# Start-up of a fused Fourier-mixing kernel: second weights loaded on ScalarE's queue, maxima found with TensorE, residual map moved, paired evacuations

## What is computed

```python
def _L0_conv_ref(x, w1, b1, w2, b2, bias_w, bias_b):      # x: (8, 32, 32, 384)
    bias = x @ bias_w.T + bias_b
    xb = x.reshape(B, H, W, nb, bs)                       # nb = 4 blocks of bs = 96 channels
    xf = jnp.fft.rfftn(xb, axes=(1, 2), norm='ortho')
    xr, xi = (xf.real, xf.imag)
    r1 = relu(_block_mul(xr, w1[0]) - _block_mul(xi, w1[1]) + b1[0])
    i1 = relu(_block_mul(xr, w1[1]) + _block_mul(xi, w1[0]) + b1[1])
    r2 = _block_mul(r1, w2[0]) - _block_mul(i1, w2[1]) + b2[0]
    i2 = _block_mul(r2, w2[1]) + _block_mul(i1, w2[0]) + b2[1]
    out = jnp.fft.irfftn(jax.lax.complex(r2, i2), s=(H, W), axes=(1, 2), norm='ortho')
    return out.reshape(B, H, W, C) + bias

x = x + _L0_conv_ref(_gn(x), ...)     # _gn: group norm, 32 groups, over pixels and channels of the group
```

## Time and profile before

| | |
|---|---|
| median of three runs | 462.18 us |
| the profiled execution, its own time | 459.74 us |
| its span, first to last instruction | 457.6 us |
| PE busy | 400.7 us (88%) |
| DVE busy | 344.6 us (75%) |
| ACT busy | 227.7 us (50%) |
| POOL busy | 66.5 us (15%) |

### The profile page before, as it was taken

The page is one execution under the profiler, slowest core; times in us unless marked ns, Lnnn a source line. Parts: engine busy times, 40 slices in busy tenths (PEclk is TensorE's granted clock), DMA queues, the critical chain, the costliest instruction groups (busy, mean ns, idle before and its releaser), DMA issues.

```text
span 457.6 us, 19262 instructions
## 1 busy us (share of the span) xinstructions
PE 400.7 (88%) x8530; PEld 355.4 (78%) x8530; DVE 344.6 (75%) x768; ACT 227.7 (50%) x504; POOL 66.5 (15%) x72
## 2 busy tenths in 40 slices
PE   4529778899899998999899998999899998995896
PEld 4418667787788988988788988988788887984794
DVE  3676988887797788868688788768787778769324
ACT  2632765326644476427643566437642575435320
POOL 0000007600060005100150006000240007000000
PEclk9758999999999999999999999999999999998899
DMA  6770000053001700052001700151002600130003
GB/s 212 212 210 0 4 1 4 2 184 130 3 5 36 278 4 4 26 178 112 4 4 50 265 4 4 35 208 73 5 3 94 221 3 4 37 140 1 4 4 138
DMA packets 12566, 33.22 MB, mean 73 GB/s; under 512 B 4994, under 2 KB 6692, under 8 KB 12484
## 3 DMA queue, kind: packets, MB, share of 16 engines
q1 hardware_dynamic: 12484, 32.00, 20.1%
HBM read 16.26 MB, written 12.58 MB: 63 GB/s over the span
## 4 chain that ended last, share of the span: by engine, by line
PE 62%; DVE 22%; issue 4%; SPq 4%; ACT 4%; DMA 2%; DVEq 0%
PE bank L552 62%; DVE r L1066 2%; DMA bias_all<-in_bias_b 2%; DVE rsum L1059 2%; DVE xs L1006 2%; DVE xs L1008 2%; DVE z L991 2%; DVE xs L1004 1%; DVE dev L1022 1%; DVE dev L1024 1%; SPq L511 1%; DVE sX L1020 1%; SPq L506 1%; DVE rho L991 1%; DVE g L1073 1%
## 5 line engine op out<-in xcount | busy, mean ns | idle before, releaser
L552 PE MATMUL bank<-biasw,y 128*64 128x384 f16 x1152 | 112.5, 339 | 4.5 <-DVE g L1073 4.4
L552 PEld LDWEIGHTS bank<-biasw,y 128*64 128x64 f16 x1152 | 94.2, 196 | 7.8 <-issue 5.2
L552 PE MATMUL bank<-w2s,rho 128*64 128x96 f16 x3072 | 83.9, 208 | 0.2 <-issue 0.2
L552 PEld LDWEIGHTS bank<-w2s,rho 128*64 128x64 f16 x3072 | 80.8, 109 | 3.6 <-issue 2.8
L907 ACT ACTIVATE z<-bank 128x384 f16<-128x384 f32 x72 | 35.2, 489 | 65.7 <-PE bank L552 65.0
L552 PE MATMUL bank<-w1R,y 128*128 128x192 f16 (+3 forms) x768 | 59.6, 228 | 1.6 <-issue 1.1
L552 PE MATMUL bank<-tab,x_sb 128*128 128x128 f32 x384 | 52.5, 290 | 9.6 <-DMA x_sb<-in_x 5.8
L991 DVE SCALAR_TENSOR_TENSOR z<-bank,z 128x384 f16<-128x384 f32 x72 | 40.0, 557 | 26.3 <-ACT z L907 25.9
L552 PEld LDWEIGHTS bank<-tab,x_sb 128*128 128x128 f32 x384 | 48.2, 201 | 14.3 <-issue 8.0
L892 ACT ACTIVATE g<-bank 128x384 f16<-128x384 f32 x64 | 31.0, 484 | 55.8 <-PE bank L552 55.7
L991 DVE SCALAR_TENSOR_TENSOR rho<-bank,rho 128x256 f16<-128x256 f32 (+2 forms) x128 | 40.1, 364 | 23.8 <-ACT rho L925 15.4
(11 more groups left out here) (104 smaller groups left out, 464.4 us busy)
## 6 DMA issues: line engine op xcount, KB each, us to landing
x_sb<-in_x SPq DMA_DIRECT2D x16, 768.0 KB, 6.8
out<-o_sb SPq DMA_DIRECT2D x14, 768.0 KB, 3.5
y<-y SPq DMA_DIRECT2D x24, 128.0 KB, 2.8
out<-o_sb SPq DMA_DIRECT2D x8, 192.0 KB, 1.9
tab<-in_tab SPq DMA_DIRECT2D x1, 672.0 KB, 5.8
o_sb<-in_bias_wt SPq DMA_DIRECT2D x4, 144.0 KB, 2.8
b1s<-in_b1h SPq DMA_DIRECT2D x1, 384.0 KB, 5.0
tab<-in_tab SPq DMA_DIRECT2D x1, 291.5 KB, 2.7
```

What stands on the lines that cost most here:

```text
L552: return nc.tensor.matmul(o, lhsT, rhs, start=start, stop=stop, **kw)
```

## The change

1. The twelve loads of `w2` are issued by ACT, ahead of its first activation. Nothing of them is left on SP's queue. `w2real` is zeroed first, so that these loads can start with those of `w1`.
2. POOL takes no part in the scales. DVE reduces to one number in each partition (`peak`), a PE product with the identity lays the 128 numbers in a row of PSUM (`peak_to_row`), DVE finds the scale in partition 0, and a PE product with ones gives it to all partitions (`top_to_all`). The constants grow by the identity, 128 columns.
3. The second maxima, the second scale and all of `second_forms` are made in the start: part 0 ahead of the first maximum, part 1 and `second_peak` ahead of `moments(0)`, `second_scales` between `scales(0)` and `y_low`.
4. The map is made inside `c1` of image 0: `shift_rows` after unit 1, the PE products ahead of unit 6, `shift_all` after unit 6.
5. POOL's `add_map(b)` waits for `scales` of image b + 1 instead of the end of `p4`, and does one image each time, image b itself (images 6 and 7 together).
6. `spectrum_sum`, `r_high` and `r_low` take two neighbouring units in one instruction where they can. All units have 128 rows; `p3_half` gets three more matmuls for that.
7. In `p4` the third `c2_bias` moves from ahead of `j` = 6 to ahead of `j` = 7.

```diff
-            sp.wait_ge(w1_zeroed, 1)
+            sp.wait_ge(w1_zeroed, 2)
...
-            sp.wait_ge(zeroed, N_ZERO)
-            with nc.allow_non_contiguous_dma(reason="one column of 96 per block"):
-                for dst, src in w2_loads():
-                    sp.dma_start(dst, src).then_inc(w2_in, 16)
...
                 if m == 0 and not first:
                     pe.wait_ge(o_ready, 8 * b)
+                    pe.wait_ge(added_ready, 6)
...
                     if u == 6:
+                        if first:
+                            pe.wait_ge(shift_in, 16 * N_SHIFT)
+                            pe.wait_ge(added_ready, 1)
+                            mm(y_bank[1][:, 0:CH], T("impulse", 2), b2rows[:, :], True, False, skip_group_check=True)
+                            for blk in range(BLOCKS):
+                                last = mm(y_bank[1][:, BC * blk:BC * blk + BC], b2row0[:, blk, :], w2imag[:, blk, :], False, blk == BLOCKS - 1, skip_group_check=True)
+                            last.then_inc(shift_prod, 1)
                         p3_half(b, 0, first)
...
-                        for slot in range(3 if t == 3 else 4):
+                        for slot in range(4):
...
-                    if j in (2, 4, 6):
-                        gi = j // 2 - 1
+                    if j in (2, 4, 7):
+                        gi = {2: 0, 4: 1, 7: 2}[j]
...
+            def peak_to_row(k):
+
+                pe.wait_ge(peak_ready, k + 1)
+                mm(c_bank[2][0:1, 0:128], peak[:, k:k + 1], T("ident"), True, True).then_inc(peak_row, 1)
+
+            def top_to_all(k):
+
+                pe.wait_ge(top_ready, k + 1)
+                mm(c_bank[2][:, 256:257], ones[:, :], top[:, k:k + 1], True, True).then_inc(top_all, 1)
...
+            peak_to_row(0)
+            second_products()
+            top_to_all(0)
             mean(0)
+            peak_to_row(1)
             variance(0)
...
+            top_to_all(1)
             image(0, 0, first=True)
...
             for b in range(BATCHES):
-                pool.wait_ge(rhol_ready, 8 * b + 8)
-                if b == 0:
-                    add_map(0)
-                if b + 1 < BATCHES:
-                    add_map(b + 1)
+                pool.wait_ge(dve_step, NSTEP * min(b + 2, BATCHES))
+                add_map(b)
...
+            act.wait_ge(w1_zeroed, 2)
+            for dst, src in w2_loads():
+                nc.scalar.dma_start(dst, src).then_inc(w2_in, 16)
             act.wait_ge(zeroed, N_ZERO)
...
+            def r_high(b, u, n=2):
+                act.wait_ge(spec_sum, 9 * b + u + n)
+                nc.scalar.activation(r[:, 0, u:u + n, :], rsum[:, u:u + n, :], ACT.Relu).then_inc(rh_ready, n)
...
+                    if u == 6:
+                        spectrum_sum(b, 0, 2)
+                    if u > 6:
                         spectrum_sum(b, u - 5)
 
-                for u in range(4):
-                    r_low(b, u)
-                spectrum_sum(b, 4)
-                spectrum_sum(b, 5)
-                if first:
-                    second_scales()
-                for u in range(6, 9):
-                    spectrum_sum(b, u)
-                    r_low(b, u - 2)
-                    if first and u == 7:
-                        bias_low(*bias_parts, bias_ready)
-                r_low(b, 7)
-                r_low(b, 8)
+                r_low(b, 0)
+                r_low(b, 2)
+                spectrum_sum(b, 4, 2)
+                spectrum_sum(b, 6, 2)
+                r_low(b, 4)
+                if first:
+                    bias_low(*bias_parts, bias_ready)
+                spectrum_sum(b, 8)
+                r_low(b, 6)
+                r_low(b, 8, 1)
...
-            first_scale()
+            second_forms(0)
+            first_peak()
+            scale_of(0, s1[:, :])
             channel_means(0)
             (w1_high, _), w1_src, w1_scale = w1_parts
             nc.vector.tensor_scalar(w1_high, w1_src, w1_scale, None, ALU.mult).then_inc(w1r_ready, 1)
+            second_forms(1)
+            second_peak()
             moments(0)
             weight_low(*w1_parts, w1r_ready)
             scales(0)
+            second_scales()
             for ct in range(NT):
                 y_low(0, 0, ct)
-            second_forms()
-            shift_rows()
-            shift_all()
             image(0, 0, first=True)
```

More of the change, by code:

```diff
@@ L165 @@
 TABW = TAB16W = 0
-for _name, _wide in (("width", 256), ("own", 128), ("block3", 128), ("const", 64), ("sign", 3), ("coef", 4), ("impulse", 128), ("row0", 128)):
+for _name, _wide in (("width", 256), ("own", 128), ("block3", 128), ("const", 64), ("sign", 3), ("coef", 4), ("impulse", 128), ("row0", 128), ("ident", 128)):
     TAB[_name] = (TABW, TABW + _wide)
@@ L210, in constants @@
     put("row0", np.broadcast_to(impulse[1], (BC, 128)))
+    put("ident", np.eye(128))
     marks = np.zeros((1, 2))
@@ L268, in spectral_block_kernel @@
         b1small = sb("b1small", [2 * BLOCKS, BC])
-        peaks1 = sb("peaks1", [128, 2])
-        peaks2 = sb("peaks2", [128, 2])
+        peak = sb("peak", [128, 2])
+        top = sb("top", [128, 2])
+        ones = sb("ones", [128, 128])
         power = sb("power", [128, 2])
@@ L314, in spec_bank @@
         def spec_bank(u):
-            return (*c_bank, y_bank[0], *b_bank[0:2], *c_bank)[u]
+            return banks[SPEC_BANKS[u]]
+        SPEC_BANKS = (5, 6, 7, 0, 2, 3, 5, 6, 7)
         p1_bank = (y_bank[1], b_bank[2])
@@ L744, in c2_rho @@
                 for half in range(2):
+                    if gi == 0 and half == 1:
+                        pe.wait_ge(rhoh_ready, 8 * b + 8)
+                        pe.wait_ge(rhol_ready, 8 * b + 8)
                     for slot, tile, k in ((0, 0, 0), (1, 1, 0), (2, 1, 1), (3, 2, 1)):
@@ L792, in image, with second_products @@
                 p6(b, range(EARLY, TILES))
+            def second_products():
+                pe.wait_ge(w2_in, 16 * N_W2)
+                for pieces in (WIDE_PIECES, SMALL_PIECES):
+                    for tile, first_row, last_row, k, ri, ch in pieces:
+                        for half in range(2):
+                            blk = 2 * half + k
+                            last = mm(w2_product(tile)[first_row:last_row, half, :], w2T[:, blk, ri, ch:ch + last_row - first_row],
+                                      w2imag[:, blk, :], True, True, skip_group_check=True)
+                last.then_inc(w2_prod, 1)
+            def peak_to_row(k):
[4 more added lines that the diff above has]
+                mm(c_bank[2][:, 256:257], ones[:, :], top[:, k:k + 1], True, True).then_inc(top_all, 1)
             pe.wait_ge(width_in, 16)
@@ L1150, in image @@
                     add_x(b, p, t)
+            nc.vector.memset(w2real[:, :, :, :], 0.0).then_inc(w1_zeroed, 1)
             nc.vector.memset(w1raw[:, :, :, :], 0.0).then_inc(w1_zeroed, 1)
-            for a in (w2real[:, :, :, :], w2f[:, :, :, :], rhoX[:, :, :, :, :], extreme[:, :], sumsq[:, :, :],
-                      r[96:128, :, 3:8:4, :]):
+            for a in (top[:, :], w2f[:, :, :, :], rhoX[:, :, :, :, :], extreme[:, :], sumsq[:, :, :]):
                 nc.vector.memset(a, 0.0).then_inc(zeroed, 1)
+            nc.vector.memset(ones[:, :], 1.0)
             nc.vector.memset(qv[:, :], 0.0).then_inc(o_ready, 8)
@@ L1205, in bias_low, with second_forms @@
                     low(dst[1][:, ct], src[:, ct], scale, dst[0][:, ct]).then_inc(ready, 1)
-            def second_forms():
-                dve.wait_ge(w2_prod, 1)
-                for part in range(2):
+            def second_forms(part):
+                if part == 0:
+                    dve.wait_ge(w2_in, 16 * N_W2)
+                    dve.wait_ge(zeroed, N_ZERO)
+                    dve.wait_ge(consts_in, 16)
+                else:
+                    dve.wait_ge(w2_prod, 1)
+                for _ in range(1):
                     for slot, tile, first_row, last_row in ((0, 0, 0, 128), (1, 1, 0, 64), (2, 1, 64, 128), (3, 2, 0, 128)):
@@ L1233, in shift_all @@
                         parts = []
-                        for v in (added[:, a, :], bias_all[:, :], c_bank[2][:, 0:CH]):
+                        for v in (added[:, a, :], bias_all[:, :], y_bank[1][:, 0:CH]):
                             if len(parts) == 0:
```

126 lines of the change are left out of this document (49 added, 77 removed).

## The result

| | before | after |
|---|---|---|
| median of four runs | 461.88 us (461.31 to 462.39) | 449.44 us (447.89 to 451.98) |
| profiled execution, its own time | 459.74 us | 451.98 us |
| its span | 457.6 us | 450.1 us |
| PE / DVE / ACT / POOL busy | 400.7 / 344.6 / 227.7 / 66.5 us | 405.1 / 312.4 / 222.1 / 82.5 us |

The ratio is 0.974 (0.969 to 0.979): 12.4 us faster, where 4.4 had been forecast, and outside the range. The profiled execution of after is the slowest of its four runs and that of before is faster than the four in the table, so this pair of traces shows 7.8 us of the 12.4. Single stages can be compared in it; totals are taken from the medians.

What follows compares the result with a forecast made beforehand. PE was taken as the bound in middle images, chains through DVE in the start and image 0. +2.8 - 0.8 - 6.3 - 0.1 = -4.4 us from 459.74 gave 455.3, as median 457.8; range 452.5 to 463.0.

Steps and rivals of the forecast that it cites:

- The bias product ahead of `j` = 7: End of p4: PE's 1.3 us wait for rhoX stays, cost nothing; at best 0.6 us, kept for the range.
- The statistics beside POOL: DVE's channel_means and moments, slowed by POOL, make PE wait for qv and g; moving POOL gains 0.8 us an image.
- `y_low` beside POOL: y_low now meets POOL's tiles, making DVE up to 3 us later at add_x; taken as hidden, cost nothing.
- POOL's new place costs: Rival: y_low loses whole tiles, add_x starts 1 us late, the 0.8 us an image comes back: 462.6 us; chance 0.07.
- Pairs: Paired sums and r_low on DVE save 0.3 us an image; added p3_half matmuls give back up to 0.1; net 0.2.
- The middle image: Statistics and pairs together: -1.0 us an image, -1.05 before rounding, -6.3 over six images.
- Image 7: Last image, no statistics: pairs save 0.4 us around r, but the first sum comes later; -0.1 us.
- The start: Up to c1 of image 0, through ACT's loads, forms and both scales: c1 at 39 us, not 36.3; +2.8 us.
- The rival of ACT's queue: Start: ACT and SP share one descriptor generator, up to 0.6 us more per ACT issue; 464 us, chance 0.13.
- Image 0: Half clock in c1 +1.5, shift products +1.7, shift_all +0.6, against -0.2, -1.1 and POOL's -3.3: -0.8 us.
- The start and the map as a whole: New start +2.8 us up to c1, plus image 0's clock and shift terms less scale and pairs, +2.5.
- more is gained: Rival: sums and r set the pace around p3 and p4, 1.6 us an image, start only 1.5; 453 us, chance 0.2.

Runs made afterwards that it cites:

- e2: The changed kernel with c2_rho again waiting for rhoX of both halves, the bias product staying ahead of j = 7; 457.83 us, 0.994 of before.
- e1: The changed kernel with the third bias product ahead of j = 6 again and the rhoX wait not split; 457.16 us, 0.992 of before.
- e5: The kernel before with POOL's edit alone: add_map(b) waits for scales of image b + 1 and does image b; 451.74 us, 0.979 of before.
- e8: The kernel before with POOL's edit, the bias product ahead of j = 7 and the rhoX wait split by halves; 441.50 us, 0.958 of before.
- e11: e10 with spectrum_sum, r_high and r_low on pairs of units as in the changed kernel; 445.11 us, 0.965 of before.
- e10: e8 with all units of 128 rows and units still single; 444.41 us, 0.964 of before.

## Why the prediction was wrong

**The step that failed** is "The bias product ahead of `j` = 7 ... I cost it at nothing". As an edit by itself that was right (`e2`). But it came with the split of the wait, which was in the kernels' difference and not in my reading of it, and the sentence "that way is as long as before" asked only when `j` = 7 is ready, not what `c2_rho` needs first. In its place the runs show 8 us over eight images in the changed kernel (`e1`), 1.0 us in a middle image (49.98 in `e1`, 48.95 in the changed kernel, the shortest of each). That is as much as the whole distance between the forecast of 457.8 and the measured 449.4; the other terms that were off went both ways.

Point by point:

- **The statistics beside POOL**: forecast 0.8 us an image, measured 1.16 (50.87 to 49.71, `e5`). The mechanism was right, and the waits for `qv` and `g` are gone. The term was taken from the visible waits alone (0.4 + 0.4); where the rest lies wasn't looked into.
- **`y_low` beside POOL**: costed at nothing, and nothing showed, though it is stretched to 1.84 us. The rival "POOL's new place costs" falls. By the Trainium skill ("SBUF — State Buffer", section "SBUF: two separate sides") the two block each other for whole instructions; the rows agree in kind, both sides are longer (1.84 and 1.56 us, and 9.72 for seven tiles). What DVE loses there lies ahead of waits that it has anyway (0.38 us for PE ahead of `add_x`), and so costs PE nothing.
- **Pairs**: forecast -0.3 us an image and +0.1 for the added rows, measured +0.25 (48.97 against 48.73) and +0.04 (48.73 against 48.69). The wrong sign: I counted DVE's fixed part. That ACT and PE get the first unit of a pair only with its second fits the place of the cost, ahead of `p4`, but which wait it is wasn't measured.
- **The middle image**: -1.16 - 1.02 + 0.04 + 0.25 = -1.89, against a forecast of -1.05 (its two terms as shown, 0.8 and 0.2, make 1.0). The shortest of after is 48.95, 1.92 less than 50.87, so the parts close for an undisturbed image. Over all six the two traces show 8.2 us, 1.37 an image, since some images of after are longer, image 1 by 3.2 us.
- **Image 7**: forecast -0.1, came -1.1. Its wait for `rhoX` went with the others.
- **The start**: forecast +2.8 with `c1` at 39, came 39.07. The steps: `yraw` at 10.8 (forecast 11), the scale on all partitions at 20.6 (20.3), `y_high` at 34.08 (33.6). That the scale was on time is luck: `w2` had landed only at 14.9 (forecast 13), so the first maximum was done at 17.9 instead of 16.2, and PE's products of `w2` took 1.75 us at a granted clock of 1.00 where I had 3.06 at half clock. The rival of ACT's queue falls: nine issues took ACT 5.46 and SP 5.53 us side by side. Before, alone, SP took 5.63 for the same nine as now and 4.99 for nine of `w2`, so no issue became dearer by 0.1 us.
- **Image 0**: forecast -0.8, came -1.05, by luck, from parts of other sizes. POOL's edit gave 2.5 (61.39 to 58.90, `e5`; forecast 3.3), PE's order 2.2 more (56.67, `e8`; forecast 0), the pairs and rows cost 1.4 (58.11, `e11`), and the new start 2.2 (60.35; forecast +2.5: 1.5 + 1.7 + 0.6 - 0.2 - 1.1). These parts are each from one trace, and image 0 scatters: it took 61.86 us in `e1` and 59.67 in `e2`, whose times are the same. The half clock lasted 3.5 us of `c1`, not 5.5.
- **The start and the map as a whole** cost 5.7 us by the start of image 1 (99.42 against 93.67 in `e11`) and about 4 by the medians. These were the edits the change began with, and they are its loss; in this the forecast was right (2.8 + 2.5).

So the forecast had the start right and the steady state at a little over half. The rival "more is gained" (453) named `rhoX` but with no mechanism.

## What to carry to other kernels

Read a wait for several results by what the first instruction behind it needs: a wait that can be split by halves, with 1.6 us of other work moved between the producer and it, gave 1 us an image here. A wait that goes may only uncover the next one: the same edit gave 0 us while DVE was late and 10 us once it was not, so edits on one ring of engines have to be tried together as well as one by one. And take a bundle apart even when it wins: here a dozen lines brought 20 us, and the other parts gave back 7.

## What the runs showed of the hardware

PE stops by itself in the small matmuls at the end of `c1`, mostly 9.4 to 9.6 us after the start of an image, for nothing that the profile shows. It does so in every kernel here, before too (0.88 us in image 1). The longest, in image 1 of after:

```profile
108.29 0.56 PE L551 MATMUL bank<-w1R,y 128*32 128x96 f16 x29
...
110.87 0.67 PE L551 MATMUL bank<-w1R,y 128*32 128x96 f16 x19 [2.02 <-issue]
```

The same gap is 0.64 us in image 3 of after, 1.13 in image 3 of `e11` and 0.84 in image 5 of `e10`, and missing in the images between. With it images of one kernel differ by 0.4 to 1.5 us, and by 3.2 us in image 1 of after; it may be part of the scatter of the runs. From 108 to 111.5 us the DMA queues of after moved this:

```profile
q1 hardware_dynamic: 43, 0.17, 11.6%
q8 instruction: 1, 0.02, 1.7%
```

One packet of instructions was fetched in that stretch. By itself it doesn't explain the stop: images 2 and 4 of after, which have none, show one packet on the same queue in the same stretch, and in image 3 of `e11`, which has one, none moves between 8.6 and 12 us after the start. Whether PE waits for instructions there was not tested; the cause is open.

The stop also costs clock: right behind it, from 110.9 to 114.3 us, the granted clock is 0.50. Such falls come at 63, 70 and 111 us in the profiled execution of after, 3.4 us each, and one of 6.8 us at 415. The first three come behind idle time of PE (2.6 us for `yraw`, 1.6 for `rho`, the 2.0 of the stop), the last within a wait of 3.1 us for `rho` in image 7. That execution is the slowest of its runs (granted clock 0.957 in the mean, 0.964 to 0.973 in the others).

Two queues that issue DMAs at once, ACT's and SP's, didn't slow each other by 0.1 us an issue (5.46 and 5.53 us for nine). The Trainium skill ("Perfetto Trace Analysis", section "DMA Instruction — HWDGE (DVE, Sync)") has the descriptor generator locked for exclusive use during an issue; in these rows at most 0.1 us an issue can be lost to that.
